# Loads ahead of the main loop shared out over two queues, and the program probabilities summed in the block that loads the weights

## What is computed

```python
def _L3_xattn_ref(builder_state, base_state, input_ids, program_probs, A, Bmat, Cmat, W_in, b_in, ...):
    ...
    _, states = jax.lax.scan(step, jnp.zeros((builder_state.shape[0], S), U.dtype), U.transpose(1, 0, 2))
    ssm_out = jnp.einsum('tbs,sh->bth', states, Cmat)
    x = residual + ssm_out
    mod = program_probs.mean(axis=1) @ W_prog.T + b_prog
    return x + mod[:, None, :]
```

## Time and profile before

| what | value |
|---|---|
| median of 3 executions | 4470.65 us (4469.39 to 4470.91) |
| the profiled execution | 4469.49 us, its span 4467.7 us |
| mean granted TensorE clock | 0.987 |
| busy: TensorE, VectorE, ACT, GpSimd | 96%, 84%, 61%, 48% of the span |
| read from and written to memory | 115.01 and 37.88 MB, 34 GB/s over the span |

### The profile page before, as it was taken

How to read it: one execution, slowest core, us unless ns; L and a number is a source line. 1 busy time by engine, 2 the same in 40 slices (tenths; PEclk the granted TensorE clock), 3 DMA queues, 4 the chain that set the end, 5 groups by cost and what they waited for, 6 DMA issues and landing times.

```text
span 4467.7 us, 111509 instructions
## 1 busy us (share of the span) xinstructions
PE 4269.0 (96%) x38182; PEld 3576.6 (80%) x38309; DVE 3766.1 (84%) x10020; ACT 2742.3 (61%) x5761; POOL 2125.0 (48%) x2084
## 2 busy tenths in 40 slices
PE   1899999999999999999999999999999999999859
PEld 1678888888888888888888888888888888888745
DVE  2579988898999899889898989899889988998734
ACT  0466666666666666666666666666666666666522
POOL 0244454455445544554455445544554455445424
PEclk9899999999999999999999999999999999999979
DMA  4001010000101000101010101010101010000037
GB/s 99 18 20 31 19 31 29 22 27 29 31 19 30 29 31 19 31 29 31 19 31 28 31 19 31 29 31 19 31 29 31 19 31 29 29 21 26 19 92 264
DMA packets 127574, 159.95 MB, mean 36 GB/s; under 512 B 23925, under 2 KB 114362, under 8 KB 122618
## 3 DMA queue, kind: packets, MB, share of 16 engines
q1 hardware_dynamic: 127034, 152.93, 11.3%
HBM read 115.01 MB, written 37.88 MB: 34 GB/s over the span
## 4 chain that ended last, share of the span: by engine, by line
PE 92%; DVE 1%; issue 1%; POOL 1%; DMA 1%; ACT 1%; DVEq 0%; SPq 0%; ACTq 0%; POOLq 0%
PE bank L622 17%; PE bank L692 13%; PE bank L630 13%; PE bank L614 8%; PE bank L662 8%; PE bank L722 6%; PE bank L803 4%; PE bank L735 4%; PE bank L717 3%; PE bank L852 2%; PE bank L768 2%; PE bank L641 2%; PE bank L841 1%; PE bank L679 1%; PE bank L868 1%; PE bank L1470 1%
## 5 line engine op out<-in xcount | busy, mean ns | idle before, releaser
L939 ACT ACTIVATE prob<-prob 128x512 f32<-128x512 f32 x1280 | 781.9, 635 | 539.7 <-DVE prob L1094 538.8
L1083 DVE TENSOR_REDUCE mx<-bank 128x4 f32<-128x512 f32 x1280 | 841.1, 679 | 68.3 <-PE bank L662 53.6
L1347 POOL TENSOR_TENSOR rs_ln<-ve_ln,half 128x2 f32<-128x2 f32 x320 | 226.4, 707 | 1389.3 <-DVE ve_ln L1062 1389.2
L929 ACT ACTIVATE turned<-bank 128x512 f32<-128x512 f32 x960 | 547.7, 598 | 543.6 <-PE bank L614 407.0
L1094 DVE TENSOR_TENSOR prob<-bank,mx 128x512 f32<-128x512 f32 x1280 | 850.2, 682 | 36.5 <-PE bank L692 7.6
L949 ACT ACTIVATE probT<-bank 128x512 f32<-128x512 f32 x1280 | 724.0, 604 | 172.1 <-PE bank L692 161.8
L692 PE MATMUL bank<-ident,prob 128*128 128x128 f32 x5120 | 735.5, 279 | 13.2 <-ACT prob L939 9.0
L692 PEld LDWEIGHTS bank<-ident,prob 128*128 128x128 f32 x5120 | 582.2, 143 | 112.4 <-issue 55.9
L622 PE MATMUL bank<-turned,shared 128*128 128x256 f32 x2560 | 614.9, 383 | 2.0 <-ACT turned L929 1.9
L622 PEld LDWEIGHTS bank<-turned,shared 128*128 128x128 f32 x2560 | 468.0, 191 | 78.7 <-issue 23.1
L1394 POOL TENSOR_SCALAR shared<-turned,half_of 128x512 f32<-128x512 f32 x256 | 400.3, 1575 | 138.3 <-ACT turned L929 138.3
(11 more groups left out here) (215 smaller groups left out, 8265.8 us busy)
## 6 DMA issues: line engine op xcount, KB each, us to landing
shared<-in_x SPq DMA_DIRECT2D x128, 256.0 KB, 3.7
CB<-in_ctx SPq DMA_DIRECT2D x64, 256.0 KB, 3.7
CC<-in_ctx SPq DMA_DIRECT2D x64, 256.0 KB, 2.7
mod<-mod_rows SPq DMA_DIRECT2D x64, 256.0 KB, 3.4
residual<-X SPq DMA_DIRECT2D x64, 256.0 KB, 3.7
out<-turned SPq DMA_DIRECT2D x16, 1024.0 KB, 4.8
turned<-residual SPq DMA_DIRECT2D x14, 1024.0 KB, 6.8
shared<-in_ctxb SPq DMA_DIRECT2D x2, 2048.0 KB, 7.3
```

The costliest lines, as they stand in the source:

```text
L929: nc.scalar.activation(dst, banks.of(f"{unit}.{name}")[:, 0:n], ACT.Copy).then_inc(*st["act"].mark(name))
L939: nc.scalar.activation(flat(t), flat(t), ACT.Exp, scale=SCALE[p]).then_inc(*st["act"].mark(f"exp.{b}{r}"))
L1083: nc.vector.tensor_reduce(m[:], banks.of(f"{att}.tile.{b}{r}")[:, :].rearrange("p (h t) -> p h t", h=4), AX, ALU.max)\
```

## The change

The row and column loads go from SP to ACT (same block). So do the loads of the two halves of the probabilities, which now stand first on ACT's queue and have a place each: the old one in `shared`, and `turned`. VectorE's memsets go to the first block, and behind them both sums, their addition and the scaling, ordered by a new semaphore `means`. The last four steps of `mod` (transpose, copy, product, addition) go from the end of the second block to its start on TensorE; on VectorE they stand behind the copy of the identity. SP's store of `mod` waits for the last of them alone.

```diff
-        ctxb_sb = shared[:, 0:S // 2 * NP].rearrange("p (s n) -> p s n", n=NP)
...
+        probs_in = [t[:, 0:S // 2 * NP].rearrange("p (s n) -> p s n", n=NP)
+                    for t in (shared, trn_all[:].rearrange("p k a w -> p (k a w)"))]
...
         with nc.Block() as block:
+            @block.vector
+            def _(dve):
+                nc.vector.memset(ones_b[:], 1.0)
...
+                nc.vector.memset(w_u[:, :, NS:128], 0.0)
+                for c in range(2):
+                    dve.wait_ge(half_in[c], 16)
+                    nc.vector.reduce_sum(msum[:, c, 0:NP], probs_in[c].rearrange("p s n -> p n s"), AX).then_inc(means, 1)
+                dve.wait_ge(means, 2)
+                nc.vector.tensor_tensor(msum[:, 0, 128:128 + NP], msum[:, 0, 0:NP], msum[:, 1, 0:NP], ALU.add).then_inc(means, 1)
+                dve.wait_ge(means, 3)
+                nc.vector.tensor_scalar(msum[:, 1, 128:128 + NP], msum[:, 0, 128:128 + NP], 1.0 / S, None, ALU.mult).then_inc(means, 1)
+
+            @block.scalar
+            def _(act):
+                n = 0
+                ctxb_v = ctxb_d.rearrange("b (c s) n -> b c s n", c=2)
+                for c in range(2):
+                    act.dma_start(probs_in[c], ctxb_v[:, c, :, :]).then_inc(half_in[c], 16)
+                for name, t in rows.items():
+                    act.dma_start(t[:], dram["row_" + name].partition_broadcast(128)).then_inc(loaded_b, 16)
+                    n += 16
+                for name, t in cols.items():
...
+                act.wait_ge(loaded_b, n)
...
             @block.sync
...
-                for name, t in rows.items():
-                    sp.dma_start(t[:], dram["row_" + name].partition_broadcast(128)).then_inc(loaded, 16)
-                    n += 16
-                for name, t in cols.items():
...
                 sp.wait_ge(loaded, n)
```

In the second block the loop over the halves and its chain of waits on `prep` are gone from VectorE, TensorE and SP; what is new there:

```diff
                 nc.vector.tensor_copy(ident_b[:], ident[:])
+                dve.wait_ge(means, 5)
+                nc.vector.tensor_copy(msT[0:NP, 0, 0:128], pbank[4][0:NP, 0:128]).then_inc(means, 1)
+                dve.wait_ge(means, 7)
+                nc.vector.tensor_tensor(mod[:, 0, :], pbank[5][:, 0:D], prog_b[:, 0, :], ALU.add).then_inc(means, 1)
...
             @block.sync
             def _(sp):
+                sp.wait_ge(means, 8)
                 sp.dma_start(mod_d, mod[:, 0, :]).then_inc(mods, 16)
+                sp.wait_ge(mods, 16)
...
             def _(pe):
+                pe.wait_ge(means, 4)
+                nc.tensor.transpose(pbank[4][0:NP, 0:128], msum[:, 1, 128:128 + NP], ident[:]).then_inc(means, 1)
+                pe.wait_ge(means, 6)
+                nc.tensor.matmul(pbank[5][:, 0:D], msT[0:NP, 0, 0:128], w_prog[0:NP, 0, :], start=True, stop=True).then_inc(means, 1)
                 pe.wait_ge(prep, 2)
```

More of the change, by code:

```diff
@@ L362, in build @@
         pbank = [ctx.enter_context(nc.psum_tensor(f"bank{n}", [128, 512], F32)) for n in range(8)]
-        loaded, prep, mods = sem("loaded"), sem("prep"), sem("mods")
+        loaded, loaded_b, prep, mods, means = (sem(n) for n in ("loaded", "loaded_b", "prep", "mods", "means"))
+        half_in = [sem(f"half_in{c}") for c in range(2)]
         steps = {u: {e: Steps(sem, u, e) for e in ENGINES} for u in UNITS}
@@ L395, in build @@
         with nc.Block() as block:
+            @block.vector
+            def _(dve):
+                nc.vector.memset(ones_b[:], 1.0)
+                nc.vector.memset(a_two[:, NS:128], 0.0)
+                nc.vector.memset(half[:], -0.5)
+                nc.vector.memset(vp1[:], 0.0)
+                nc.vector.memset(vp2[:], 0.0)
+                nc.vector.memset(vp3[:], 0.0)
+                nc.vector.memset(w_u[:, :, NS:128], 0.0)
[16 more added lines that the diff above has]
+                for name, t in cols.items():
+                    if name not in ("q3_b", "k3_b"):
+                        act.dma_start(t[:], dram["col_" + name]).then_inc(loaded_b, 16)
+                        n += 16
+                        continue
+                    for r in range(4):
+                        for m in range(DH):
+                            d = 64 * r + 32 * m
+                            act.dma_start(t[32 * r:32 * r + 32, m:m + 1],
+                                         dram["col_" + name][d % 128:d % 128 + 32, d // 128:d // 128 + 1],
+                                         allow_slow_non_contiguous=True).then_inc(loaded_b, 16)
+                            n += 16
+                act.wait_ge(loaded_b, n)
             @block.sync
@@ L465, in _ @@
                 nc.vector.tensor_tensor(rows["v3_b"][:], rows["v3_b"][:], pbank[1][:, 0:D], ALU.add)
-                nc.vector.memset(w_u[:, :, NS:128], 0.0)
                 nc.vector.tensor_copy(w_u[:, :, 0:NS], pbank[2][:, 0:DH * NS].rearrange("p (a n) -> p a n", a=DH)).then_inc(prep, 1)
@@ L475, in _ @@
                 last.then_inc(prep, 1)
[L477 to L488, removed]
             @block.sync
             def _(sp):
[L492 to L498, removed]
+                sp.wait_ge(means, 8)
                 sp.dma_start(mod_d, mod[:, 0, :]).then_inc(mods, 16)
-                sp.wait_ge(mods, 48)
+                sp.wait_ge(mods, 16)
             @block.tensor
             def _(pe):
+                pe.wait_ge(means, 4)
+                nc.tensor.transpose(pbank[4][0:NP, 0:128], msum[:, 1, 128:128 + NP], ident[:]).then_inc(means, 1)
+                pe.wait_ge(means, 6)
+                nc.tensor.matmul(pbank[5][:, 0:D], msT[0:NP, 0, 0:128], w_prog[0:NP, 0, :], start=True, stop=True).then_inc(means, 1)
                 pe.wait_ge(prep, 2)
@@ L523, in _ @@
                 last.then_inc(prep, 1)
[L524 to L527, removed]
         NB = 4
```

## The result

| | before | changed |
|---|---|---|
| median of the executions | 4470.23 us (4469.39 to 4470.91, 4 runs) | 4441.55 us (4439.9 to 4445.5, 4 runs) |
| ratio, 95% interval | | 0.9937 (0.992 to 0.9954) |
| the profiled execution, its span | 4469.49, 4467.7 | 4445.5, 4443.7 |
| second block starts | 53.33 | 51.79 |
| loop's first load | 95.53 | 66.64 |

The change gains 0.6%. "The loop" stands for everything from the loop's first load to the end, so the fourth block is in it. The profiled execution was the slowest of the four. Its two blocks and its loop give the whole difference: 1.5 us from the first block, 27.4 from the second, 4.9 us lost in the loop: 4469.5 - 1.5 - 27.4 + 4.9 = 4445.5.

A forecast was written before the change was run, and what follows sets the result against it. SP's issue was taken to bind the first block and TensorE the loop. The sum was 4469.5 - 7.4 (first block) - 27.1 (second block), loop 0, = 4435.0 us profiled, 4436 as a median; range 4422 to 4447.

The forecast's parts named there:

- the rival given 0.20: First block: weights starved or halves landing late, so the block gains about 0; time 4443, chance 0.20.
- the one given 0.48: The forecast itself: first block bound by transfer work, ending at 45.5 us; median 4436 us, chance 0.48.
- First block, the loads: Loads shared between SP and ACT: 43.5 us of transfer work ends at 45.5, gain 7.4 us, bounds 0 and about 20.
- The weights starve: First block: 128 B weight pieces wait behind halves and rows, SP's issue follows; block end 52.5, time 4443; 0.20 with late halves.
- land late: First block: second half lands with the last weight at 45, its sum ends at 53; 4443, counted within the 0.20.
- The queues overlap: First block: rows wait on something besides the engines, weights pass meanwhile; block ends at 33 to 35, time 4425, chance 0.25.
- Issue time "usually small": Skill rule for the first block's loads: issuing from two engines saves only sequencer time, usually small relative to the DMA.
- The rival that rested on it, 64.4 us: First block already bound by transfers: it ends at 64.4 us, a loss of 11.1 there; time 4454, chance 0.04.
- VectorE in the first block: Seven memsets and both sums moved there, 18 us; the second sum over at 31 or 32, hidden under the loads.
- Second block: Sums and the wait between them leave the path; the block goes from 42.2 to 15.1 us, gain 27.1 us.
- The loop: Main loop, not edited: change taken as 0, with 7.4 us either way for one stretch of low TensorE clock.
- Slower than before: First block: small packets get dearer when engines change between two queues, needing 43 ns more each; chance 0.02.

The follow-up runs named there:

- Halves alone: The changed kernel with rows and columns back on SP's queue behind the weights, the halves still loaded by ACT in the first block: 4453.2 us.
- rows alone: The kernel before with only the rows and columns moved to ACT's queue, the halves still serial in the second block: 4459.04 us.
- the second one: The profiled execution when the changed kernel itself was measured once more, unedited: 4444.62 us over 5 runs, profiled loop 4374.2 us.

## Why the prediction was right or wrong

The measured 4441.55 us lies in the range of 4422 to 4447, and the change is faster, as said. The forecast of 4436 came out 5.5 us low. In the profiled execution, for which the sum was made, it was 4435.0 against 4445.5: 5.9 us too little for the first block, 4.9 for the loop, 0.3 too much for the second block. The case that happened in the first block is the rival given 0.20, not the one given 0.48.

- *First block, the loads, "I take 45.5, all the engines' work laid end to end".* This is the step that failed: the start came at 51.8, the gain was 1.5 us, not 7.4. The work was sized rightly (42.4 us up to 49 against 43.5). What was wrong is the sentence that two queues "should seldom lack work". They took turns packet by packet, SP's queue got 3.7% of the engines while the halves passed (4 to 12 us) and 9.6% while the rows did (15 to 25), and when those were through, one queue was left with 19 us of issue (29.87 to 48.78) at 0.82 of the engines. Halves alone and rows alone each showed it. The passage to the next block was short as well, 0.4 us: behind its last issue SP waited 2.6 us for `NF` to land.
- *The weights starve.* Its mechanism holds, and its numbers: block end at 52.5 forecast, 51.4 found; 4443 forecast, 4441.55 found. The closeness is in part luck. It had all of SP's 28 us of issue come after the rows; in fact eight pieces went out meanwhile, and from 28.32 on 20.5 us were left, with 2.6 for the landing. And 4445.5, the profiled execution, holds 4.9 us of the loop. The halves did not land late.
- *The queues overlap.* Its premise, that the rows wait on something that isn't the engines, was right (47 ns a 1 KB packet when the packets read different rows, 126 when they read one). What didn't follow is that weights pass meanwhile.
- *Issue time "usually small" (the Trainium skill, "DMA: Bandwidth & Descriptors", Issuing engines are not separate DMA queues).* In this block issue was what bound, before and at the end after: with rows and columns on a second queue and nothing else changed, the start fell from 53.33 to 40.64. The rival that rested on it, 64.4 us, is out.
- *VectorE in the first block.* Sums over by 22.3 us, bound given 32. Hidden.
- *Second block.* 14.85 us to the first load for 15.1; 27.4 us gained for 27.1. What these rest on held: the chain in front took 2.5 us (51.79 to 54.24), and the store was hidden.
- *The loop.* Taken as 0 with 7.4 us either way. It lost 4.9 us in the profiled execution, 2.1 in the second one, 3.4 on the mean of all runs. The reason given for the margin, one stretch of low clock in the first groups, covers at most the 1.7 us lost there; 2.3 us were lost where the clock never fell. The profiled 4445.5 us is still inside the range, by 1.5.
- *Slower than before.* Small packets did not get dearer by the 43 ns it needed: those of 128 B took 13 ns on the mean in both kernels.

## What to carry to other kernels

Here two queues that share the DMA engines took turns by packet, so the queue with the small packets was slowed by the ratio of packet times, not by half: 128 B packets of 13 ns beside 1 KB packets of 126 ns got a tenth of the engines. So look at the packet sizes on both queues before sharing loads out, and give the slowed queue less issue. A row read by 128 partitions from one address made slow packets: reading it once and spreading it on chip brought the block's end forward by 11 us. Work that waits for nothing but its own load (here the sums) can stand beside the loads, and its cover can be read straight from the timeline; but its load is not free there. The halves took 7.6 us of the first block alone and 11.2 beside the rows, for the 27.4 us gained in the second.

## What the runs showed that was not expected

The turns were of exactly one packet, 1187 to 1195 over 10 us, and 2548 to 2553 over 7 us with faster row packets. Most packets of a row that is read 128 times are no slower than others (46 ns at the median); four in ten take over 100 ns and make the cost. The two halves slowed the other queue by an amount that a trace of either alone doesn't show: 7.6 us for 11 us of transfers. In the kernels that spread the rows on chip TensorE's products took 14 us (16.98 to 30.97), and they and VectorE's copies, over by 36.1, stayed under the loads. And a loop whose code was not touched became 3.4 us longer on the mean, of which the clock explains a part at most.
